# Feed-forward gate and linear part in three rounded passes instead of float32, in one phase of a four-layer model

## The chip, the cores and the metric

The kernel runs on one core of a Trainium2 chip. The metric is the device time of one execution in microseconds (us). A profiled execution also has a span, from its first recorded instruction to its last, and of this span the hardware profiler keeps every instruction of five engines: PE (TensorE, with PEld for its weight loads), DVE (VectorE), ACT (ScalarE), POOL (GpSimd) and SP (SyncE, which here issues transfers).

## The reference

Four layers run on 8 sequences of 512 tokens with 128 channels. The change is in the second half of the first layer, a small transformer of six layers, each an attention over windows of 32 tokens with 16 heads, followed by this feed-forward part (DIM 128, hidden width 341):

```python
def ffn_layer(x, g, bln, W1, b1, W2, b2):
    mu = x.mean(-1, keepdims=True)
    var = ((x - mu) ** 2).mean(-1, keepdims=True)
    xn = (x - mu) / jnp.sqrt(var + 1e-05) * g + bln
    hg = xn @ W1 + b1                       # 128 -> 682
    a, gate = jnp.split(hg, 2, -1)          # linear part, gate
    return a * jax.nn.gelu(gate, approximate=False) @ W2 + b2
```

All inputs and outputs are float32.

## The kernel before, in words

The phase concerned is `local_transformer_phase`. Six layers of 8 sequences of 4 tiles of 128 tokens give 192 tiles, and each engine runs one written-out loop `for k in range(-2, ALL + 8)`, whose order is the order of the program on that engine. Semaphores that are counted up per tile or per sequence tie the engines together; an engine waits in program order, so that all behind a wait stands still with it. In iteration k the kernel scores tile k, projects values for k+1 and queries and keys for k+2, and finishes k-1.

The feed-forward part of sequence n is spread over iterations: with t = k % 4, the sequence just ended is turned at t == 1 (`ffn_turn`), gets mean and deviation at t == 1 and 2 (`ffn_stats`, `ffn_shift`), and at t == 3 is turned back (`ffn_back`), scaled by ACT (`scale_norm`, which writes `xn`, 128 channels x 512 tokens) and multiplied with the gate half of W1 (`ffn_gate`). The linear half (`ffn_a`) follows at t == 0, the product with W2 at t == 1 and 2. Both halves have 341 columns in chunks of 128, 128 and 85 (`HCH`): the first chunk stands ahead of the second half of the attention-weighted values (`weigh_values(k, 1)`), the other two behind it.

At t == 3 the order is as follows, and the names are those used below. PE: scores, `ffn_back`, projections, `turn_out`, projection of keys, `turn_probs` (waits for ACT's exponentials), `turn_qk` (waits for `copy_out` of ACT), `weigh_values` first half, `project_out`, gate chunk 0, `weigh_values` second half, gate chunks 1 and 2, and then the scores of the next iteration. ACT: `scale_norm`, `square`, `exponentials`, `copy_out`, `square`, `copy_probs`, two `copy_qk`, `gelus`. DVE: `centre`, two `products`, `sum_squares`, `divide`, `sum_squares`, `add_output`, `divide`. POOL: `normalise` and then `rotate` for keys and queries, four additions of 128x512 that start when PE's `turn_qk` is through.

Float32 operands of a matmul count as one instruction in the program and leave two records in the trace. The projections of this phase already work in another way: `product` makes three matmuls of operands in the format float32r (`F32R`), of which one is a rounded value (hi) and the other its remainder (lo): hi x hi, hi x lo and lo x hi. ACT rounds (`nc.scalar.copy` to an F32R tile), and DVE or POOL subtracts to get the remainder.

W1 of a layer comes by one transfer in `load_ffn`, issued in the seventh iteration of a layer after the last sequence of the layer before is done, and `scale_norm` waits for it.

Of the kernel before, what the change touches and what calls it, by code (L numbers as in the profile page):

```python
# [8 lines left out]
F32 = mybir.dt.float32  # L9
# [7 lines left out]
P = 128  # L17
SEQS = 8
# [1126 lines left out]
def local_transformer_phase(nc, g, name, w):  # L1145
# [20 lines left out]
    def body(ph):  # L1166
# [4 lines left out]
        wo = sb("wo", [P, CH, P])  # L1171
        w1 = sb("w1", [P, 2 * HIDDEN])
        w2 = sb("w2", [P, 3, P])
# [32 lines left out]
        y_hat = sb("y_hat", [P, TOKENS])  # L1206
        xn = sb("xn", [P, TOKENS])
        gates = sb("gates", [P, 3, TOKENS])
        table_pick = sb("table_pick", [P, 3])
        bank = ph.ps("bank", [P, 8, TOKENS])  # L1210
# [6 lines left out]
        per_seq = {"ffn_turned": 1, "ffn_back": 1, "gate_done": 3, "a_done": 3, "w2_done": 2,  # L1217
                   "ys_hi_ready": 1, "y_tok_ready": 1, "xn_ready": 1, "gelu_done": 3,
                   "stats_ready": 1, "aggregated": 1, "var_ready": 1, "y_hat_ready": 1, "shift_ready": 1, "prod_ready": 3, "seq_done": 2,
# [3 lines left out]
        vals_loaded = [ph.sem(f"vals_loaded{i}") for i in range(2)]  # L1223
        split_hi, split_lo = ph.sem("split_hi"), ph.sem("split_lo")
        masks_ready, tables_ready, pads_ready = ph.sem("masks_ready"), ph.sem("tables_ready"), ph.sem("pads_ready")
        CONST_LOADS, FFN_LOADS = 16 * 4, 16 * 11
        PE_MADE = ("scores_done", "v_projected", "qk_projected", "probs_turned", "qk_turned", "out_turned", "pv_done", "wo_done",
                   "ffn_turned", "ffn_back", "gate_done", "a_done", "w2_done")
        ACT_MADE = ("exp_done", "v_copied", "squared", "probs_t_ready", "qkt_copied", "out_copied", "ys_hi_ready", "y_tok_ready", "y_hat_ready", "xn_ready", "gelu_done",
                    "logs_ready", "inv_norms_ready")  # L1230
        DVE_MADE = ("max_ready", "centred", "products_ready", "norms_ready", "sums_inverted", "att_ready", "y_added",
                    "stats_ready", "aggregated", "var_ready", "shift_ready", "prod_ready", "seq_done")
        POOL_MADE = ("rotated", "norms_guarded", "qk_normed", "ys_ready", "rstd_ready")
# [43 lines left out]
        with nc.Block() as block:  # L1277

            @block.sync
            def _(sp):  # L1280
# [13 lines left out]
                def load_ffn(layer):  # L1294
                    sp.wait_ge(q["seq_done"], seq("seq_done", layer * SEQS - 1))
                    sp.dma_start(w1[:], w["W1"][layer]).then_inc(ffn_loaded, 16)
                    sp.dma_start(w2[:, 0:2], w["W2"][layer, 0:2 * P].rearrange("(c p) d -> p c d", p=P)).then_inc(ffn_loaded, 16)
                    sp.dma_start(w2[0:HIDDEN - 2 * P, 2], w["W2"][layer, 2 * P:HIDDEN]).then_inc(ffn_loaded, 16)
                    for i, key in enumerate(("ln_g", "ln_b", "b2")):
                        sp.dma_start(ln[:, i:i + 1], w[key][layer].unsqueeze(1)).then_inc(ffn_loaded, 16)  # L1300
                    for side in range(2):
                        at = side * HIDDEN
                        sp.dma_start(b1[:, 3 * side:3 * side + 2], w["b1"][layer, at:at + 2 * P].rearrange("(c p) -> p c", p=P),
                                     allow_slow_non_contiguous=True).then_inc(ffn_loaded, 16)
                        sp.dma_start(b1[0:HIDDEN - 2 * P, 3 * side + 2:3 * side + 3], w["b1"][layer, at + 2 * P:at + HIDDEN].unsqueeze(1)).then_inc(ffn_loaded, 16)
                    sp.nop().then_inc(ffn_loaded, 16)
# [33 lines left out]
            def _(pe):  # L1340
# [145 lines left out]
                def ffn_back(n, k):  # L1486
# [4 lines left out]
                    last.then_inc(q["ffn_back"], 1)  # L1491

                def ffn_gate(n, k, chunks):
                    if 0 in chunks:
                        pe.wait_ge(q["xn_ready"], seq("xn_ready", n))
                        pe.wait_ge(ffn_loaded, FFN_LOADS * (n // SEQS + 1))
                        after_qk(k)
                    else:
                        pe.wait_ge(q["seq_done"], seq("seq_done", n - 1))
                    for i in chunks:  # L1500
                        h0, hn = HCH[i]
                        nc.tensor.matmul(bank[0:hn, FFN_HIDDEN[i], :], w1[:, HIDDEN + h0:HIDDEN + h0 + hn], xn[:], start=True, stop=True).then_inc(q["gate_done"], 1)

                def ffn_a(n, k, chunks):
                    if 0 in chunks:
                        after_qk(k)
                    for i in chunks:
                        h0, hn = HCH[i]
                        pe.wait_ge(q["gelu_done"], seq("gelu_done", n, i + 1))
                        nc.tensor.matmul(bank[0:hn, FFN_HIDDEN[i], :], w1[:, h0:h0 + hn], xn[:], start=True, stop=True).then_inc(q["a_done"], 1)  # L1510

# [49 lines left out]
            def _(act):  # L1561
# [62 lines left out]
                def copy_turned(n):  # L1624
                    act.wait_ge(q["ffn_turned"], seq("ffn_turned", n))
                    act.wait_ge(q["y_hat_ready"], seq("y_hat_ready", n - 1))
                    for odd in range(2):
                        last = nc.scalar.copy(y_tok[:].rearrange("p (t a d) -> p t a d", a=2, d=HD)[:, :, odd, :],
                                              bank[:, FFN_TURN[odd], 0:TILES * HD].rearrange("p (t d) -> p t d", d=HD))
                    last.then_inc(q["y_tok_ready"], 1)  # L1630
# [9 lines left out]
                def scale_norm(n):  # L1640
# [3 lines left out]
                    nc.scalar.activation(xn[:], bank[:, FFN_BACK, :], ACT.Identity, bias=ln[:, 1:2], scale=ln[:, 0:1]).then_inc(q["xn_ready"], 1)  # L1644

                def gelus(n):
                    nc.scalar.activation(table_pick[:, 1:2], table_pick[:, 0:1], ACT.Gelu)
                    act.wait_ge(q["w2_done"], seq("w2_done", n - 1))
                    for i, (h0, hn) in enumerate(HCH):
                        act.wait_ge(q["gate_done"], seq("gate_done", n, i + 1))  # L1650
                        nc.scalar.activation(gates[0:hn, i, :], bank[0:hn, FFN_HIDDEN[i], :], ACT.Gelu, bias=b1[0:hn, 3 + i:4 + i]).then_inc(q["gelu_done"], 1)
# [8 lines left out]
                for k in range(-2, ALL + 8):  # L1660
# [8 lines left out]
                    if is_tile(k):  # L1669
                        exponentials(k)  # L1670
                    if is_tile(k - 1):
                        copy_out(k - 1)
# [80 lines left out]
            def _(dve):  # L1753
# [65 lines left out]
                def ffn_stats(n):  # L1819
# [9 lines left out]
                    nc.vector.tensor_scalar(var_eps[:], mean_var[:, :, 1], LN_EPS, None, ALU.add).then_inc(q["var_ready"], 1)  # L1829

                def ffn_shift(n):
                    dve.wait_ge(q["rstd_ready"], seq("rstd_ready", n))
# [17 lines left out]
                for k in range(-2, ALL + 8):  # L1850
# [7 lines left out]
                    if t == 2 and is_seq(n - 1):  # L1858
                        ffn_shift(n - 1)
                    if is_tile(k):  # L1860
                        divide(k, 0)
# [599 lines left out]
```

## Time and profile before

| what | value |
|---|---|
| median of 3 runs | 4583.93 us (4583.06 to 4589.22) |
| the profiled execution, its own time | 4596.79 us |
| span of the profiled execution | 4595.0 us |
| PE busy over the span | 4112.4 us (89%) |
| DVE, ACT, POOL busy over the span | 3218.4, 2632.4 and 2429.1 us |

The phase with the change takes most of the span, roughly from 370 to 3560 us. A busy share is the time in which an engine works on something. For PE, records of matmuls overlap, since they are pipelined, so that the distance from one start to the next tells what a matmul costs, and not its recorded length. "Idle" is the time ahead of an instruction in which its engine had nothing to do, with what ended it. The columns of the rows are explained where they stand.

### The profile page before, as it was taken

Reading aid. Unit: us, or ns where it says so; the run is one execution under the profiler, and the core shown is the slowest. Engines: PE = TensorE matmul, PEld = TensorE weight load, DVE = VectorE, ACT = ScalarE, POOL = GpSimd, SP = SyncE. Lnnn points to the kernel's source line nnn. Section 1 sums busy time; section 2 is a strip of 40 time slices with the busy share of each in tenths; the row PEclk is TensorE's granted clock in tenths of the full one; section 3 lists DMA queues with packets and bytes.
Section 4 is the critical chain, followed back from the end, with each engine's and each line's share of the span. In section 5 each row is a group of like instructions: output and inputs, shape, how many; then the busy total and the mean of one; then the engine's idle time right before and its main releaser. Section 6 shows DMA issues by size and latency. Waiting matters only on the chain. (4 is left out here: it accounts for less than half of the span.)

```text
span 4595.0 us, 167423 instructions
## 1 busy us (share of the span) xinstructions
PE 4112.4 (89%) x70858; PEld 3335.7 (73%) x71050; DVE 3218.4 (70%) x5446; ACT 2632.4 (57%) x4318; POOL 2429.1 (53%) x1973
## 2 busy tenths in 40 slices
PE   6886999999999999999999999999998759668767
PEld 6885777777777777777777777777776449558457
DVE  4557777877778777877778777777775564564554
ACT  2324666666665666566666666666665437546445
POOL 3335665666566556656666566655663227517026
PEclk9997999999999999999999999999999869878878
DMA  1003222232222222232222222222221021221122
GB/s 27 0 0 92 68 68 69 58 90 69 69 66 78 69 68 67 61 85 71 67 70 77 71 67 68 70 62 70 68 66 44 10 64 49 72 63 44 28 67 77
DMA packets 214267, 281.83 MB, mean 61 GB/s; under 512 B 58926, under 2 KB 103764, under 8 KB 212788
## 3 DMA queue, kind: packets, MB, share of 16 engines
q1 hardware_dynamic: 199796, 249.82, 20.6%
q0 software_dynamic: 9536, 19.55, 1.6%
q8 instruction: 555, 9.09, 0.8%
q10 hardware_dynamic: 4224, 2.10, 0.2%
q14 instruction: 156, 1.28, 0.1%
HBM read 54.95 MB, written 18.28 MB: 16 GB/s over the span
## 5 line engine op out<-in xcount | busy, mean ns | idle before, releaser
L1717 POOL TENSOR_TENSOR local_normed<-local_rot,local_sines 128x512 f32<-128x512 f32 x768 | 954.8, 1279 | 837.4 <-PE local_bank L1429 832.9
L1727 POOL TENSOR_TENSOR local_normed<-local_normed,local_inv_norm 128x1024 f32<-128x1024 f32 x384 | 734.2, 1934 | 273.8 <-ACT local_inv_norm L1617 273.8
L1794 DVE TENSOR_TENSOR local_rot<-local_bank,local_table 128x1024 f32<-128x1024 f32 x384 | 470.2, 1224 | 399.9 <-ACT local_squares L1598 393.3
L1347 PE MATMUL local_bank<-local_wqkv_hi,local_ys_hi 128*128 128x512 f32 x1152 | 493.5, 428 | 33.9 <-issue 22.0
L1593 ACT COPY local_v_tile<-local_bank 128x1024 f32<-128x1024 f32 x192 | 195.1, 1016 | 545.0 <-PE local_bank L1349 545.0
L1794 DVE TENSOR_TENSOR local_sines<-local_bank,local_table 128x1024 f32<-128x1024 f32 x384 | 466.1, 1214 | 0.0
L1800 DVE TENSOR_REDUCE local_norm<-local_squares 128x16 f32<-128x1024 f32 x384 | 463.8, 1208 | 0.0
L1349 PE MATMUL local_bank<-local_wqkv_hi,local_ys_lo 128*128 128x512 f32 x1152 | 456.8, 397 | 0.0
L1348 PE MATMUL local_bank<-local_wqkv_lo,local_ys_hi 128*128 128x512 f32 x1152 | 454.7, 395 | 0.0
L1598 ACT ACTIVATE local_squares<-local_bank 128x1024 f32<-128x1024 f32 x384 | 397.0, 1034 | 76.9 <-PE local_bank L1349 76.9
L1781 DVE TENSOR_REDUCE local_top<-local_bank 128x16 f32<-128x1024 f32 x192 | 234.8, 1223 | 239.3 <-PE local_bank L1377 238.8
L1467 PE MATMUL local_bank<-local_att_t,local_wo 128*128 128x128 f32 x3072 | 391.6, 280 | 8.3 <-issue 2.9
L1467 PEld LDWEIGHTS local_bank<-local_att_t,local_wo 128*128 128x128 f32 x3072 | 359.2, 192 | 35.8 <-issue 18.1
L1429 PE MATMUL local_bank<-ident,local_normed 128*128 128x128 f32 x3072 | 374.1, 275 | 4.6 <-POOL local_normed L1727 4.1
L1455 PEld LDWEIGHTS local_bank<-local_vals,local_probs_t 64*32 64x32 f32 x24576 | 271.6, 105 | 138.9 <-issue 125.8
L1455 PE MATMUL local_bank<-local_vals,local_probs_t 64*32 64x65 f32 x24576 | 341.3, 225 | 18.9 <-issue 17.1
L1429 PEld LDWEIGHTS local_bank<-ident,local_normed 128*128 128x128 f32 x3072 | 334.0, 142 | 24.2 <-POOL local_normed L1727 5.2
L1377 PEld LDWEIGHTS local_bank<-local_k_t,local_q_t 64*32 64x32 f32 x24576 | 258.6, 105 | 115.0 <-issue 114.4
L1377 PE MATMUL local_bank<-local_k_t,local_q_t 64*32 64x64 f32 x24576 | 297.2, 226 | 25.6 <-issue 25.0
L1347 PEld LDWEIGHTS local_bank<-local_wqkv_hi,local_ys_hi 128*128 128x128 f32 x1152 | 219.2, 190 | 84.9 <-issue 36.0
L1810 DVE TENSOR_TENSOR local_att<-local_bank,local_inv_sum 128x512 f32<-128x512 f32 x384 | 265.4, 691 | 13.2
L1349 PEld LDWEIGHTS local_bank<-local_wqkv_hi,local_ys_lo 128*128 128x128 f32 x1152 | 219.0, 190 | 50.8
(406 smaller groups left out, 8821.5 us busy)
## 6 DMA issues: line engine op xcount, KB each, us to landing
local_vals<-local_v_tile SPq DMA_DIRECT2D x1152, 130.0 KB
local_vals<-local_v_tile SPq DMA_DIRECT2D x672, 65.0 KB
local_stage<-in_L_ffn_Wqkv SPq DMA_DIRECT2D x6, 1536.0 KB, 7.7
moe_w<-in_L_ffn_W SPq DMA_DIRECT2D x3, 2048.0 KB, 9.7
x_rows<-moe_rows SPq DMA_DIRECT2D x24, 256.0 KB, 4.6
moe_w<-y_rows SPq DMA_DIRECT2D x24, 256.0 KB, 5.3
local_wo<-in_L_ffn_Wo SPq DMA_DIRECT2D x6, 512.0 KB
moe_taken<-x_rows,moe_take POOLq DMA_INDIRECT x149, 2.6
```

What stands on the lines that cost most here:

```text
L1347: nc.tensor.matmul(out, hi, wqkv_hi[:, d0:d1], start=True, stop=False)
L1348: nc.tensor.matmul(out, hi, wqkv_lo[:, d0:d1], start=False, stop=False)
L1349: return nc.tensor.matmul(out, lo, wqkv_hi[:, d0:d1], start=False, stop=True)
L1377: last = nc.tensor.matmul(bank[b * BLOCK:(b + 1) * BLOCK, SCORES[odd], c * WIN:(c + 1) * WIN], q_t[rows, c, b * BLOCK:(b + 1) * BLOCK], k_ ...
L1429: last = nc.tensor.transpose(bank[:, QK_TURN[a][j // 4], j % 4 * P:(j % 4 + 1) * P], normed[:, (8 * a + j) * P:(8 * a + j + 1) * P], g.ide ...
L1455: last = nc.tensor.matmul(bank[b * BLOCK:(b + 1) * BLOCK, WEIGHED[i][odd], j * (HD + 1):(j + 1) * (HD + 1)], probs_t[rows, c, b * BLOCK:(b ...
L1467: last = nc.tensor.matmul(bank[:, WO_BANK, 0:P], wo[:, c, :], att_t[:, c, :], start=(c == 0), stop=(c == CH - 1))
L1598: nc.scalar.activation(squares[:, a * INNER:(a + 1) * INNER], two(QK[a]), ACT.Square).then_inc(q["squared"], 1)
L1717: last = nc.gpsimd.tensor_tensor(of_heads(normed, a)[:, :, to], of_heads(rot, a)[:, :, to], of_heads(sines, a)[:, :, of], ALU.add)
L1727: nc.gpsimd.tensor_tensor(of_heads(normed, a), of_heads(normed, a), inv_norm[:, a * HEADS:(a + 1) * HEADS].unsqueeze(2).to_broadcast([P, H ...
L1794: last = nc.vector.tensor_tensor(of_heads(out, a), src, table[:, m % TILES, row, :].unsqueeze(1).to_broadcast([P, HEADS, HD]), ALU.mult)
L1800: nc.vector.tensor_reduce(norm2[:, cols], of_heads(squares, a), AX, ALU.add).then_inc(q["norms_ready"], 1)
```

## The change

Gate and linear part are computed from split operands, as the projections are. Per sequence, ACT rounds `xn` into `xn_hi` and DVE writes the remainder `xn_lo` (`split_norm` on both); once in each of the six layers, at its first sequence, the same is done with W1 (`split_w1`). Each float32 matmul of `ffn_gate` and `ffn_a` becomes three (`in_three`). `xn` has no tile of its own any more and lies in `y_tok`; W1 is loaded into the tile of the gates. PE waits for the remainders ahead of gate chunk 0 (before: for `xn`).

```diff
-        w1 = sb("w1", [P, 2 * HIDDEN])
+        w1_hi, w1_lo = (sb(n, [P, 2 * HIDDEN], F32R) for n in ("w1_hi", "w1_lo"))
...
-        xn = sb("xn", [P, TOKENS])
+        xn = y_tok
+        xn_hi, xn_lo = (sb(n, [P, TOKENS], F32R) for n in ("xn_hi", "xn_lo"))
         gates = sb("gates", [P, 3, TOKENS])
+        w1 = gates[:].rearrange("p c t -> p (c t)")[:, 0:2 * HIDDEN]
...
+                def in_three(out, cols):
+
+                    nc.tensor.matmul(out, w1_hi[:, cols], xn_hi[:], start=True, stop=False)
+                    nc.tensor.matmul(out, w1_lo[:, cols], xn_hi[:], start=False, stop=False)
+                    return nc.tensor.matmul(out, w1_hi[:, cols], xn_lo[:], start=False, stop=True)
+
                 def ffn_gate(n, k, chunks):
                     if 0 in chunks:
-                        pe.wait_ge(q["xn_ready"], seq("xn_ready", n))
-                        pe.wait_ge(ffn_loaded, FFN_LOADS * (n // SEQS + 1))
+                        pe.wait_ge(q["xn_split"], seq("xn_split", n))
+                        pe.wait_ge(w1_split, n // SEQS + 1)
                         after_qk(k)
...
-                        nc.tensor.matmul(bank[0:hn, FFN_HIDDEN[i], :], w1[:, HIDDEN + h0:HIDDEN + h0 + hn], xn[:], start=True, stop=True).then_inc(q["gate_done"], 1)
+                        in_three(bank[0:hn, FFN_HIDDEN[i], :], slice(HIDDEN + h0, HIDDEN + h0 + hn)).then_inc(q["gate_done"], 1)
...
-                        nc.tensor.matmul(bank[0:hn, FFN_HIDDEN[i], :], w1[:, h0:h0 + hn], xn[:], start=True, stop=True).then_inc(q["a_done"], 1)
+                        in_three(bank[0:hn, FFN_HIDDEN[i], :], slice(h0, h0 + hn)).then_inc(q["a_done"], 1)
...
                 def copy_turned(n):
                     act.wait_ge(q["ffn_turned"], seq("ffn_turned", n))
                     act.wait_ge(q["y_hat_ready"], seq("y_hat_ready", n - 1))
+                    act.wait_ge(q["xn_split"], seq("xn_split", n - 1))
...
+                def split_norm(n):
+                    act.wait_ge(q["xn_ready"], seq("xn_ready", n))
+                    nc.scalar.copy(xn_hi[:], xn[:]).then_inc(q["xn_hi_ready"], 1)
+
+                def split_w1(layer):
+                    act.wait_ge(ffn_loaded, FFN_LOADS * (layer + 1))
+                    act.wait_ge(q["a_done"], seq("a_done", layer * SEQS - 1))
+                    nc.scalar.copy(w1_hi[:], w1).then_inc(w1_hi_ready, 1)
+
                 def gelus(n):
...
+                    if n % SEQS == 0:
+                        act.wait_ge(w1_split, n // SEQS + 1)
...
                     if is_tile(k):
                         exponentials(k)
+                    if t == 3 and is_seq(n - 1):
+                        split_norm(n - 1)
+                        if (n - 1) % SEQS == 0:
+                            split_w1((n - 1) // SEQS)
                     if is_tile(k - 1):
                         copy_out(k - 1)
...
+                def split_norm(n):
+                    dve.wait_ge(q["xn_hi_ready"], seq("xn_hi_ready", n))
+                    nc.vector.tensor_tensor(xn_lo[:], xn[:], xn_hi[:].bitcast(F32), ALU.subtract).then_inc(q["xn_split"], 1)
+
+                def split_w1(layer):
+                    dve.wait_ge(w1_hi_ready, layer + 1)
+                    nc.vector.tensor_tensor(w1_lo[:], w1, w1_hi[:].bitcast(F32), ALU.subtract).then_inc(w1_split, 1)
+
...
                     if t == 2 and is_seq(n - 1):
                         ffn_shift(n - 1)
+                    if t == 3 and is_seq(n - 1):
+                        split_norm(n - 1)
+                        if (n - 1) % SEQS == 0:
+                            split_w1((n - 1) // SEQS)
                     if is_tile(k):
                         divide(k, 0)
```

On ACT, at t == 3 of the first sequence of a layer, before the change (`local_xn` is the scaled row, `local_att_t` is what `copy_out` writes):

```order
L1644 ACTIVATE local_xn<-local_bank,local_ln 128x512
L1598 ACTIVATE local_squares<-local_bank 128x1024
L1586 ACTIVATE local_scores<-local_scores 128x1024
L1622 COPY local_att_t<-local_bank 128x1024
L1598 ACTIVATE local_squares<-local_bank 128x1024
```

and with the change, where the scaled row goes to `local_y_tok`:

```order
L1654 ACTIVATE local_y_tok<-local_bank,local_ln 128x512
L1607 ACTIVATE local_squares<-local_bank 128x1024
L1595 ACTIVATE local_scores<-local_scores 128x1024
L1658 CAST local_xn_hi<-local_y_tok 128x512
L1663 CAST local_w1_hi<-local_gates 128x682
L1631 COPY local_att_t<-local_bank 128x1024
L1607 ACTIVATE local_squares<-local_bank 128x1024
```

The rounding of the row stands between the exponentials and `copy_out`; in the other seven sequences of a layer the cast of 682 columns is not there. On DVE at the same place, with the change (before, the first and the fourth of these rows stand next to each other):

```order
L1825 TENSOR_REDUCE local_norm2<-local_squares 128x16
L1858 TENSOR_TENSOR local_xn_lo<-local_y_tok,local_xn_hi 128x512
L1862 TENSOR_TENSOR local_w1_lo<-local_gates,local_w1_hi 128x682
L1831 RECIPROCAL local_inv_sum<-local_bank 128x8
L1835 TENSOR_TENSOR local_att<-local_bank,local_inv_sum 128x2x4x64
```

The remainders follow the first `sum_squares`, which itself follows both `products`. On PE the gate before:

```order
L1467 MATMUL local_bank<-local_att_t,local_wo 128x128 x8
L1502 MATMUL local_bank<-local_xn,local_w1 128x512
L1455 MATMUL local_bank<-local_vals,local_probs_t 32x65 x32
L1502 MATMUL local_bank<-local_xn,local_w1 128x512
L1502 MATMUL local_bank<-local_xn,local_w1 85x512
L1370 MATMUL local_bank<-local_band8,local_ident16 128x512 x2
```

and with the change:

```order
L1470 MATMUL local_bank<-local_att_t,local_wo 128x128 x8
L1498 MATMUL local_bank<-local_xn_hi,local_w1_hi 128x512
L1499 MATMUL local_bank<-local_xn_hi,local_w1_lo 128x512
L1500 MATMUL local_bank<-local_xn_lo,local_w1_hi 128x512
L1458 MATMUL local_bank<-local_vals,local_probs_t 32x65 x32
L1498 MATMUL local_bank<-local_xn_hi,local_w1_hi 128x512
L1499 MATMUL local_bank<-local_xn_hi,local_w1_lo 128x512
L1500 MATMUL local_bank<-local_xn_lo,local_w1_hi 128x512
L1498 MATMUL local_bank<-local_xn_hi,local_w1_hi 85x512
L1499 MATMUL local_bank<-local_xn_hi,local_w1_lo 85x512
L1500 MATMUL local_bank<-local_xn_lo,local_w1_hi 85x512
```

Nothing has changed its place on PE; three instructions stand for one, and what the first of them waits for is another event.

## Rows read from the trace of the kernel before

**Rows 1.** Stretch, length; PE, PEld, DVE, ACT, POOL busy; granted clock, DMA share, GB/s.

```profile
500.00:3500.00 3000.00, 2913.09 (x60776) 2309.31 (x60960) 2331.92 (x3106) 1880.58 (x2530) 1815.38 (x1418) 1.00 0.27 70
```

**Rows 2.** Timeline of PE: start, length, line, out<-in, count, idle before.

```profile
1032.15 0.47 PE L1347 MATMUL local_bank<-local_wqkv_hi,local_ys_hi 128*128 128x512 f32 x1
1032.46 0.39 PE L1348 MATMUL local_bank<-local_wqkv_lo,local_ys_hi 128*128 128x512 f32 x1
1032.69 0.40 PE L1349 MATMUL local_bank<-local_wqkv_hi,local_ys_lo 128*128 128x512 f32 x1
...
1034.77 1.94 PE L1429 MATMUL local_bank<-ident,local_normed 128*128 128x128 f32 x16
...
1037.52 2.02 PE L1467 MATMUL local_bank<-local_att_t,local_wo 128*128 128x128 f32 x16
1039.38 1.02 PE L1502 MATMUL local_bank<-local_xn,local_w 128*128 128x512 f32 x2
1040.33 0.86 PE L1455 MATMUL local_bank<-local_vals,local_probs_t 64*32 64x65 f32 x64
1041.12 1.98 PE L1502 MATMUL local_bank<-local_xn,local_w 128*128 128x512 f32 x4
1042.09 0.59 PE L1502 MATMUL local_bank<-local_xn,local_w 128*85 128x512 f32 x1
1042.52 0.59 PE L1502 MATMUL local_bank<-local_xn,local_w 128*85 128x512 f32 x1
1043.16 0.38 PE L1370 MATMUL local_bank<-local_band,local_ident 128*128 128x512 bf16 x1
...
1057.30 1.98 PE L1510 MATMUL local_bank<-local_xn,local_w 128*128 128x512 f32 x4
1059.33 0.38 PE L1370 MATMUL local_bank<-local_band,local_ident 128*128 128x512 bf16 x1
```

**Rows 3.** Timeline of ACT in the same iteration.

```profile
1032.66 1.07 ACT L1586 ACTIVATE local_scores<-local_scores 128x1024 f32<-128x1024 f32 x1
1033.61 1.02 ACT L1622 COPY local_att_t<-local_bank 128x1024 f32<-128x1024 f32 x1
1034.50 1.06 ACT L1598 ACTIVATE local_squares<-local_bank 128x1024 f32<-128x1024 f32 x1
```

**Rows 4.** Two lines of the expert phases: count, shortest/median/longest ns, first and last start.

```profile
L285 ACT CAST moe_wt_hi<-moe_w x149: 617/619/657, 3784.9 to 4564.6; 128x512 fp32r x149
...
L569 DVE TENSOR_TENSOR moe_wt_lo<-moe_w,moe_wt_hi x149: 691/692/766, 3787.1 to 4565.3; 128x512 fp32r<-128x512 f32 x149
```

**Rows 5.** Timeline of DVE in the iteration of rows 2.

```profile
1037.86 1.21 DVE L1800 TENSOR_REDUCE local_norm<-local_squares 128x16 f32<-128x1024 f32 x1
1038.98 0.20 DVE L1806 RECIPROCAL local_inv_sum<-local_bank 128x8 f32<-128x8 f32 x1
```

**Rows 6.** The line of `ffn_shift` on DVE, columns as in rows 4.

```profile
L1833 DVE SCALAR_TENSOR_TENSOR local_shift<-local_mean_var,local_rstd x48: 161/760/949, 498.5 to 3545.9; 128x4 f32<-128x4 f32 x48
```

**Rows 7.** Timeline of DVE and POOL, at t == 2 and t == 3.

```profile
1024.38 0.77 DVE L1833 SCALAR_TENSOR_TENSOR local_shift<-local_mean_var,local_rstd 128x4 f32<-128x4 f32 x1
...
1021.39 4.97 POOL L1717 TENSOR_TENSOR local_normed<-local_rot,local_sines 128x512 f32<-128x512 f32 x4 [2.10 <-PE local_bank L1429]
...
1035.98 4.98 POOL L1717 TENSOR_TENSOR local_normed<-local_rot,local_sines 128x512 f32<-128x512 f32 x4 [4.04 <-PE local_bank L1429]
```

**Rows 8.** Timeline of DVE and POOL where the projection weights are split.

```profile
371.16 3.49 DVE L1775 TENSOR_TENSOR local_wqkv_lo<-local_stage,local_wqkv_hi 128x1024 fp32r<-128x1024 f32 x3
...
1401.77 5.76 DVE L1775 TENSOR_TENSOR local_wqkv_lo<-local_stage,local_wqkv_hi 128x1024 fp32r<-128x1024 f32 x2
...
1401.58 4.87 POOL L1727 TENSOR_TENSOR local_normed<-local_normed,local_inv_norm 128x1024 f32<-128x1024 f32 x2
```

**Rows 9.** An idle time of PE, and the stretch behind it, columns as in rows 1.

```profile
1553.29 0.68 PE L1377 MATMUL local_bank<-local_k_t,local_q_t 64*32 64x64 f32 x44 [2.10 <-issue]
...
1555.00:1558.00 3.00, 3.00 (x8) 2.32 (x7) 1.45 (x2) 0.98 (x2) 0.00 (x0) 0.50 0.00 0
```

More of the change, by code:

```diff
@@ L1217, in body @@
         per_seq = {"ffn_turned": 1, "ffn_back": 1, "gate_done": 3, "a_done": 3, "w2_done": 2,
-                   "ys_hi_ready": 1, "y_tok_ready": 1, "xn_ready": 1, "gelu_done": 3,
+                   "ys_hi_ready": 1, "y_tok_ready": 1, "xn_ready": 1, "xn_hi_ready": 1, "xn_split": 1, "gelu_done": 3,
                    "stats_ready": 1, "aggregated": 1, "var_ready": 1, "y_hat_ready": 1, "shift_ready": 1, "prod_ready": 3, "seq_done": 2,
@@ L1224, in body @@
         split_hi, split_lo = ph.sem("split_hi"), ph.sem("split_lo")
+        w1_hi_ready, w1_split = ph.sem("w1_hi_ready"), ph.sem("w1_split")
         masks_ready, tables_ready, pads_ready = ph.sem("masks_ready"), ph.sem("tables_ready"), ph.sem("pads_ready")
@@ L1228, in body @@
                    "ffn_turned", "ffn_back", "gate_done", "a_done", "w2_done")
-        ACT_MADE = ("exp_done", "v_copied", "squared", "probs_t_ready", "qkt_copied", "out_copied", "ys_hi_ready", "y_tok_ready", "y_hat_ready", "xn_ready", "gelu_done",
+        ACT_MADE = ("exp_done", "v_copied", "squared", "probs_t_ready", "qkt_copied", "out_copied", "ys_hi_ready", "y_tok_ready", "y_hat_ready", "xn_ready", "xn_hi_ready", "gelu_done",
                     "logs_ready", "inv_norms_ready")
         DVE_MADE = ("max_ready", "centred", "products_ready", "norms_ready", "sums_inverted", "att_ready", "y_added",
-                    "stats_ready", "aggregated", "var_ready", "shift_ready", "prod_ready", "seq_done")
+                    "xn_split", "stats_ready", "aggregated", "var_ready", "shift_ready", "prod_ready", "seq_done")
         POOL_MADE = ("rotated", "norms_guarded", "qk_normed", "ys_ready", "rstd_ready")
@@ L1295, in load_ffn @@
                     sp.wait_ge(q["seq_done"], seq("seq_done", layer * SEQS - 1))
-                    sp.dma_start(w1[:], w["W1"][layer]).then_inc(ffn_loaded, 16)
+                    sp.dma_start(w1, w["W1"][layer]).then_inc(ffn_loaded, 16)
                     sp.dma_start(w2[:, 0:2], w["W2"][layer, 0:2 * P].rearrange("(c p) d -> p c d", p=P)).then_inc(ffn_loaded, 16)
```

## The prediction

> **What bounds the kernel now.** I read the busy times by stretch first. In the phase with the change PE works 2913 of 3000 us at the full granted clock (1.00, that is 2.4 GHz), and DVE, the next, 2332 [rows 1]. So here nearly every microsecond that PE gains or stands still is one of the kernel, unless another engine is late right behind it. Next I read the timelines of one iteration with t == 3, which I take for all 48. The reader is to see how close ACT is to PE there: `copy_out` (L1622) ends at 1033.61 + 1.02 = 1034.63, and PE's `turn_qk` (L1429) starts at 1034.77 [rows 2, 3]. It is released by that copy, with 0.14 us from the end of the one to the start of the other. Ahead of the gate there is little room on DVE too: the first `sum_squares` gives way to the next instruction at 1038.98, and PE starts the gate at 1039.38 [rows 2, 5].
>
> **What the matmuls save.** In each half (gate, linear part) the two PE stretches take 1040.33 - 1039.38 = 0.95 us for one matmul (two records) and 1043.16 - 1041.12 = 2.04 us for two; in the linear part the latter is 1059.33 - 1057.30 = 2.03 [rows 2]. Together 2.99 us, of which six records at a spacing of 0.43 (1042.09 to 1042.52) are 2.58 and 0.41 are changeovers: 0.09 behind the first stretch, 0.11 at the head of the second, 0.21 behind it.
>
> The projections show three-pass matmuls of the same 128x512 shape: 0.31 us from the first start to the next, then 0.23 [rows 2]. With three and six passes that is 0.31 + 2 x 0.23 = 0.77 and 0.31 + 5 x 0.23 = 1.46, together 2.23 if no other changeover is left. If 0.09 and 0.21 behind them stay (they belong to what follows: small weight tiles, then bf16), and the second head costs 0.03 more, it is 2.56. So a half gains 0.43 to 0.76 us, a sequence 0.87 to 1.5, and 48 sequences 42 to 73 us. I take 0.88 a sequence: the gaps are in the trace at just these two places, and nothing shows them to go. That the last chunk is 85 wide changes nothing, as its records are as far apart as the others'.
>
> **The rounding on ACT.** 48 casts of 128x512, each between the exponentials and `copy_out`. The same cast in the expert phases takes 617 ns [rows 4], and an ACT instruction starts about 0.1 us before the end of the one ahead (1034.50 against 1034.63) [rows 3], so 0.52 us of ACT's time; the bounds are 0.5 and 0.64. Queued behind it are `copy_out`, the second `square`, `copy_probs` and both `copy_qk`. PE waits for the first of these already, so `turn_qk` and all behind it start 0.52 us later: PE reaches the gate at 1039.90. DVE's second `products` wait for the second `square`, so `sum_squares` shifts by 0.52 as well, and POOL's `rotate`, released by `turn_qk`, too.
>
> **The remainder on DVE.** The subtraction may start at 1038.98 + 0.52 = 1039.50 and takes 0.69 us where POOL leaves it alone [rows 4]. Here POOL is in `rotate`. Where DVE reads two SBUF operands against POOL, the trace shows what happens: `ffn_shift`, four elements wide, has a median of 760 ns and a minimum of 161 [rows 6]. It starts 2.99 us into `rotate` and ends at 1025.15 [rows 7], that is 3.76 in, or 3.60 before its own 0.16: it had to wait until the third of POOL's four additions was over. The split of the projection weights says the same: three subtractions of 128x1024 take 3.49 us without POOL, and two take 5.76 beside two operations of POOL, the first of which began 0.19 us ahead of them [rows 8]. Our subtraction starts 1039.50 - (1035.98 + 0.52) = 3.00 us into `rotate`, at the very place of `ffn_shift` one iteration earlier. It gets its turn 3.60 us in, at 1040.10, ends at 1040.79, and PE, 0.14 later, starts the gate at 1040.93 instead of 1039.90: a wait of 1.03 us. The bounds of this wait: 0.43 with no contention (0.69 in place of 1.29), and 1.7 if DVE has to stand by for one whole addition of 1.25 us.
>
> The Trainium skill says on "SBUF — State Buffer", section "SBUF: two separate sides", that the port pair of DVE and GpSimd is "an exclusive lock, not a bandwidth split": who starts first keeps it for the whole instruction. The trace agrees: 4 elements cost 0.6 us more, which a shared bandwidth would not do. Were the ports shared in proportion, the subtraction would take half of the weights' 2.9 us and the wait would be 1.2 us, which adds 7 us to the sum below.
>
> Behind the gate DVE still has `divide`, `sum_squares`, `add_output` and `divide`, some 3.2 us, before the next scores, for which PE needs 0.86 + 0.79 + 1.69 = 3.3 us from the gate; the half of `divide` that the scores wait for comes first. I count nothing there, nor for the shared tiles: `y_tok` is read by DVE long before `xn` overwrites it, W1 arrives under the same wait and as early as before, and the new waits of `copy_turned` and `gelus` are met before ACT comes to them: the one a whole iteration earlier, the other by the gate that `gelus` waits for in any case.
>
> **A usual sequence.** 0.52 + 1.03 - 0.88 = +0.67 us; 42 of them +28 us.
>
> **The first sequence of a layer (6 of them).** ACT also casts 682 columns of W1: 0.65 us more (between 0.52 for 512 and some 0.95 for 1024), so `turn_qk` is 1.17 late and PE is at the gate at 1040.55. DVE ends the row's remainder at 1040.79 + 0.65 = 1041.44. POOL's fourth addition (1.25 us) has been waiting and takes its turn; then W1 needs 0.87 (682 columns, between 0.69 and 1.16), to about 1043.5, and PE starts at 1043.65: a wait of 3.1 us (1.3 without contention). PE after such a stop: behind an idle time of 2.10 us the granted clock lies at 0.50 (1.2 GHz) over a whole 3 us [rows 9], which costs half of some 3.4 us, 1.7 us. Sum 1.17 + 3.1 + 1.7 - 0.88 = 5.1, six times +31 us.
>
> **Sum.** +28 + 31 = +59 us, less about 5 where PE comes to the gate late anyway by an idle time of its instruction supply, as in rows 9. The profiled 4596.79 us would become 4651; the median of the runs lies 12.9 below that execution, so I predict 4583.93 + 54 = 4638 us.
>
> **Rivals.**
> - The forecast, 0.62: PE waits twice in each iteration with t == 3; 4615 to 4665.
> - Both waits as forecast, but the changeovers vanish (1.5 a sequence) and the clock holds. Against it: the gaps and the clock seen. 42 x 0.05 + 6 x 2.8 = +19, so 4603. 0.15.
> - DVE takes its operands at once. For it: the subtraction is short. Against it: the wait of four elements [rows 6, 7]. 42 x (0.52 + 0.43 - 0.88) + 6 x (1.17 + 1.3 - 0.88) = +3 + 10, so 4597, or 4567 with the larger gain of the matmuls. 0.09.
> - Faster: both stops are made good behind the gate, because PE would have stood still there anyway (for its instructions, or for DVE at the next scores), and the gain of the matmuls alone is left: 4511 to 4542. It decides if PE has 1.5 us of idle time per sequence to give. For it: PE is idle for 87 of 3000 us [rows 1], some 1.9 in each 65. Against it: in the iteration shown the start of each group follows the one ahead without a gap from 1037.52 to 1043.16 [rows 2]. 0.08.
> - Much slower: the clock falls in each sequence, as two stops of 0.5 and 1.0 us lie close together. Against it: it is the full clock over the stretch in spite of many idle times near 1 us. 42 x 1.7 = +71 more, 4709. 0.06.
>
> **How the numbers follow.** 4638 is the likeliest case. The range for 8 in 10 runs from 4594, just below the case without contention, to 4668, which is the upper bound of DVE's wait (42 x 0.67 = 28 more). A measurement of this kernel can tell 0.2%, 9 us, from no change. Faster by more: 0.09 (the fourth rival and a corner of the third). Within it: 0.09 (most of the third, and a part of the second). Slower: 0.82.
>
> **What would show it.** In the profile of the changed kernel, at t == 3: nine matmul records per half, 0.23 us apart; PE's `turn_qk` released by ACT's `copy_out`, whose start lies 1.47 us behind that of the exponentials (now 0.95); the subtraction of 128x512 on DVE near 1.3 us long and not 0.69; an idle time of PE of about 1 us ahead of the first gate matmul, released by DVE, 48 times, and near 3 us in six of them, with a lower clock behind; PE's total idle time in the phase up by some 75 us and its busy time down by 40. I am wrong if the subtraction takes 0.7 us, if PE does not wait at the gate, or if the linear part, too, gets a wait.

## The result, and the profile after

The changed kernel takes 4645.35 us (median of 4 runs, 4639.33 to 4651.82), the kernel before beside it 4583.58 us (4583.06 to 4589.22). The ratio is 1.0121 with a 95% interval of 1.0104 to 1.0138: slower by 62 us, and 7 us above the forecast time of 4638. The profiled execution of the changed kernel took 4649.19 us, with a span of 4647.4 us.

The three-pass products sit at L1498, L1499 and L1500, for the gate as for the linear part. The rounding of `local_xn` on ACT is L1658 and that of W1 L1663; the remainders on DVE are L1858 and L1862. Other lines have moved: `turn_qk` is L1432 (was L1429), `copy_out` L1631 (L1622), the scores begin at L1373 (L1370).

The first view is that of busy times from 500 to 3500 us, with the columns of [rows 1].

```profile
500.00:3500.00 3000.00, 2841.33 (x59808) 2313.95 (x59971) 2345.38 (x3102) 1871.62 (x2533) 1802.72 (x1391) 0.99 0.28 68
```

In the same 3000 us PE is busy for 72 us less than in [rows 1], so it stands still for 72 us more. DVE gains 13 us and is still far from full: nothing is short of capacity, PE only stands still more often. The waits say where. They follow for PE from 500 to 3620 us: what waited, for what, us in total, times, longest.

```profile
PE local_bank L1498 <- DVE local_xn_lo L1858: 32.2, 39, 2.3
PE local_bank L1432 <- ACT local_att_t L1631: 23.4, 47, 1.1
PE local_bank L1498 <- issue: 16.1, 6, 2.7
```

Together they make 71.7 us, and none of the three stood among the waits before. `turn_qk` waits for `copy_out` in 47 sequences, and the gate for DVE's remainder. The third row is the first sequence of each of six layers; the wait there is for DVE as well (below), although the view puts it down to PE's own issue.

A usual sequence on PE follows, with start, duration, engine, line, operation and operands; the bracket is the idle time ahead and what ended it.

```profile
1115.56 1.09 PE L1419 MATMUL local_bank<-ident,local_scores 128*128 128x128 f32 x8
1117.07 1.94 PE L1432 MATMUL local_bank<-ident,local_normed 128*128 128x128 f32 x16 [0.42 <-ACT local_att_t L1631]
1118.94 0.86 PE L1458 MATMUL local_bank<-local_vals,local_probs_t 64*32 64x65 f32 x64
1119.81 2.02 PE L1470 MATMUL local_bank<-local_att_t,local_wo 128*128 128x128 f32 x16
1122.63 0.50 PE L1498 MATMUL local_bank<-local_xn_hi,local_w_hi 128*128 128x512 f32 x1 [0.80 <-DVE local_xn_lo L1858]
1122.97 0.39 PE L1499 MATMUL local_bank<-local_xn_hi,local_w_lo 128*128 128x512 f32 x1
1123.20 0.40 PE L1500 MATMUL local_bank<-local_xn_lo,local_w_hi 128*128 128x512 f32 x1
1123.53 0.86 PE L1458 MATMUL local_bank<-local_vals,local_probs_t 64*32 64x65 f32 x64
1124.32 0.50 PE L1498 MATMUL local_bank<-local_xn_hi,local_w_hi 128*128 128x512 f32 x1
```

The row of L1432 answers to `turn_qk` in [rows 2], which had no idle time ahead that the view shows, and that of the first L1498 to the first L1502. From `project_out` (L1470) to the gate it was 1.86 us; it is 2.82 here. In the linear part of the same sequence nothing waits, and the same distance is shorter than before, 1.78 us:

```profile
1136.57 2.02 PE L1470 MATMUL local_bank<-local_att_t,local_wo 128*128 128x128 f32 x16
1138.35 0.48 PE L1498 MATMUL local_bank<-local_xn_hi,local_w_hi 128*128 128x512 f32 x1
...
1141.28 0.40 PE L1500 MATMUL local_bank<-local_xn_lo,local_w_hi 128*85 128x512 f32 x1
1141.75 0.38 PE L1373 MATMUL local_bank<-local_band,local_ident 128*128 128x512 bf16 x1
```

So the wait at the gate is 2.82 - 1.78 = 1.04 us; against the gate's place in the kernel before it is 2.82 - 1.86 = 0.96. Next ACT, DVE and POOL in the same iteration, which answer to [rows 3], [rows 5] and [rows 7].

```profile
1114.44 1.06 ACT L1595 ACTIVATE local_scores<-local_scores 128x1024 f32<-128x1024 f32 x1
1115.39 0.63 ACT L1658 CAST local_xn_hi<-local_y_tok 128x512 fp32r<-128x512 f32 x1
1115.90 1.03 ACT L1631 COPY local_att_t<-local_bank 128x1024 f32<-128x1024 f32 x1
```

```profile
1120.16 1.21 DVE L1825 TENSOR_REDUCE local_norm<-local_squares 128x16 f32<-128x1024 f32 x1
1121.28 1.29 DVE L1858 TENSOR_TENSOR local_xn_lo<-local_y_tok,local_xn_hi 128x512 fp32r<-128x512 f32 x1
1122.50 0.20 DVE L1831 RECIPROCAL local_inv_sum<-local_bank 128x8 f32<-128x8 f32 x1
```

```profile
1118.29 5.43 POOL L1742 TENSOR_TENSOR local_normed<-local_rot,local_sines 128x512 f32<-128x512 f32 x4 [5.48 <-PE local_bank L1432]
```

The rounding moves `copy_out` from 0.95 to 1.46 us behind the exponentials. The subtraction starts 2.99 us into POOL's four additions, is 1.29 us long and ends 4.28 us in; the additions themselves go from 4.98 to 5.43 us.

In the first sequence of a layer DVE has the remainder of W1 behind that of the row, and PE starts the gate at its end:

```profile
1052.30 1.29 DVE L1858 TENSOR_TENSOR local_xn_lo<-local_y_tok,local_xn_hi 128x512 fp32r<-128x512 f32 x1
1053.52 1.92 DVE L1862 TENSOR_TENSOR local_w_lo<-local_gates,local_w_hi 128x682 fp32r<-128x682 f32 x1
```

```profile
1050.83 2.02 PE L1470 MATMUL local_bank<-local_att_t,local_wo 128*128 128x128 f32 x16
1055.53 0.77 PE L1498 MATMUL local_bank<-local_xn_hi,local_w_hi 128*128 128x512 f32 x1 [2.68 <-issue]
1056.10 0.63 PE L1499 MATMUL local_bank<-local_xn_hi,local_w_lo 128*128 128x512 f32 x1
1056.52 0.63 PE L1500 MATMUL local_bank<-local_xn_lo,local_w_hi 128*128 128x512 f32 x1
```

The subtraction of W1 ends at 1055.44 and the gate begins at 1055.53, 4.70 us behind `project_out`. Its passes lie 0.42 apart and not 0.23: the clock is at its lower level (0.50, that is 1.2 GHz), as the windows (length, PE busy, granted clock, DMA share, GB/s) show.

```profile
1054.00:1056.00 2.00, 0.47 (x1) 0.75 0.00 0
1056.00:1058.00 2.00, 2.00 (x67) 0.50 0.00 0
1058.00:1060.00 2.00, 2.00 (x24) 0.50 0.14 33
1060.00:1062.00 2.00, 1.75 (x12) 0.54 0.19 42
```

### The profile page after: what moved, and what is told of

It is laid out like the page before. It is cut to its first block and busy times, and to the rows that moved or that the text cites. A ratio compares the mean times of both kernels' runs of the same rounds, so it can differ in the third digit from the quotient of the medians.

```text
span 4647.4 us, 168115 instructions
## 1 busy us (share of the span) xinstructions
PE 4094.8 (88%) x71146; PEld 3391.0 (73%) x71338; DVE 3279.4 (71%) x5500; ACT 2660.0 (57%) x4372; POOL 2448.6 (53%) x1973
## 3 DMA queue, kind: packets, MB, share of 16 engines
q1 hardware_dynamic: 199796, 249.82, 21.3%
q14 instruction: 157, 1.29, 0.1%
## 5 line engine op out<-in xcount | busy, mean ns | idle before, releaser
L1742 POOL TENSOR_TENSOR local_normed<-local_rot,local_sines 128x512 f32<-128x512 f32 x768 | 976.3, 1305 | 849.7 <-PE local_bank L1432 845.2
L1470 PE MATMUL local_bank<-local_att_t,local_wo 128*128 128x128 f32 x3072 | 394.7, 282 | 10.8 <-DMA local_wo<-in_L_ffn_Wo 4.5
L1432 PE MATMUL local_bank<-ident,local_normed 128*128 128x128 f32 x3072 | 375.0, 275 | 27.8 <-ACT local_att_t L1631 23.4
L1470 PEld LDWEIGHTS local_bank<-local_att_t,local_wo 128*128 128x128 f32 x3072 | 362.3, 193 | 37.3 <-issue 10.1
L1432 PEld LDWEIGHTS local_bank<-ident,local_normed 128*128 128x128 f32 x3072 | 335.0, 142 | 52.3 <-issue 33.1
```

The costliest lines, as they stand in the source:

```text
L1432: last = nc.tensor.transpose(bank[:, QK_TURN[a][j // 4], j % 4 * P:(j % 4 + 1) * P], normed[:, (8 * a + j) * P:(8 * a + j + 1) * P], g.ide ...
L1470: last = nc.tensor.matmul(bank[:, WO_BANK, 0:P], wo[:, c, :], att_t[:, c, :], start=(c == 0), stop=(c == CH - 1))
L1742: last = nc.gpsimd.tensor_tensor(of_heads(normed, a)[:, :, to], of_heads(rot, a)[:, :, to], of_heads(sines, a)[:, :, of], ALU.add)
```

## The experiments

For each kernel the table has the distances between the starts of the scores (the first bf16 mask matmul that the trace records) of one tile and of the next, read from PE's timeline of the profiled execution, and summed: 47 tiles with the gate, 47 with the linear part (the first of each lies ahead of the first gate), and 96 others. It keeps apart where time goes, which a median of whole runs can't. The others differ by up to 11 us from before, with both signs, so single digits there mean little. A profiled execution can also lie up to 13 us from the median of its kernel (before: 4596.79 against 4583.93; remainder early: 4569.69 against 4582.48), so the sums and the ratios need not agree to 10 us.

| kernel | with gate | with linear part | others | sum | ratio to before (95%) |
|---|---|---|---|---|---|
| before | 825.4 | 761.6 | 1516.9 | 3103.9 | |
| changed | 897.9 | 740.3 | 1523.4 | 3161.6 | 1.0121 (1.0104 to 1.0138) |
| passes alone | 809.0 | 741.7 | 1517.7 | 3068.4 | 0.9932 (0.9919 to 0.9945) |
| cast alone | 851.7 | 760.9 | 1509.2 | 3121.8 | 1.0055 (1.0042 to 1.0067) |
| remainder early | 829.1 | 741.7 | 1516.6 | 3087.4 | 0.9998 (0.9989 to 1.0007) |
| W1 once | 877.3 | 741.6 | 1518.3 | 3137.2 | 1.0091 (1.0078 to 1.0104) |
| cast early | 867.3 | 741.8 | 1527.1 | 3136.2 | 1.0068 (1.0052 to 1.0083) |
| both early | 798.0 | 745.5 | 1528.2 | 3071.7 | 0.9924 (0.9910 to 0.9938) |
| norm early, old passes | 818.9 | 761.8 | 1513.1 | 3093.8 | 0.9979 (0.9970 to 0.9989) |

The median of the kernel before was 4584.29 us beside the first four experiments (17 runs) and 4592.1 beside the last three (17 runs), so ratios are the better comparison across the two.

The theory under test is that of the prediction: cheaper products (about -40 us), against two separate waits, one behind the rounding on ACT and one for the remainder on DVE, the latter long because POOL works beside it. The rivals are that the products gain nothing here, that one wait covers the other, or that the slower first sequences are what counts.

**Passes alone.** The three passes stay, what feeds them goes: ACT scales the row straight into `xn_hi`, no remainder of it is made, the third pass takes `xn_hi` again, and PE waits for the scaled row as it did before. So the output is not the full one.

```
-    return nc.tensor.matmul(out, w1_hi[:, cols], xn_lo[:], ...)
+    return nc.tensor.matmul(out, w1_hi[:, cols], xn_hi[:], ...)
...
-    nc.scalar.activation(xn[:], bank[:, FFN_BACK, :], ...)
+    nc.scalar.activation(xn_hi[:], bank[:, FFN_BACK, :], ...)
...
-    split_norm(n - 1)              # ACT and DVE
-    if (n - 1) % SEQS == 0:
+    if n - 1 == 0:
         split_w1(...)
```

> The three passes alone: ACT scales the row straight into the rounded tile, no remainder of the row is made (the third pass multiplies the rounded row again), and W1 is split in the first layer only and then kept; so remainders and the later layers' W1 are left out. My theory: PE gains 0.37 us in the gate and 0.46 in the linear part of each sequence and nothing stands against it, 48 x 0.83 = 40 us below the kernel before, 4544 us; no idle time of PE ahead of the gate, turn_qk as before at 0.14 us behind copy_out. Rival one (changeovers vanish without the waits): 73 us below, 4511. Rival two (the gain is swallowed by another wait behind the gate or by the supply of instructions): 4580 or more.

Measured: 4555.84 us, 28 us below before by the medians and 31 by the ratio (interval 25 to 37), so less than expected. In the trace the sum of the tiles falls by 35.5: 16.4 with the gate, 19.9 with the linear part, nothing in the others. Once, in layer 0, the split of W1 is still in it. That the products are faster on the chip is shown; the expected 40 us lie just above the interval.

**Cast alone.** The kernel before, and ACT writes a rounded `local_xn` that nobody reads.

```
...
+    def split_norm(n):
+        act.wait_ge(q["xn_ready"], seq("xn_ready", n))
+        nc.scalar.copy(xn_hi[:], xn[:])
...
+    if t == 3 and is_seq(n - 1):
+        split_norm(n - 1)          # between exponentials and copy_out
```

> The kernel before with nothing but a cast of the row on ACT, 128x512, between the exponentials and copy_out, into a tile that nobody reads. My theory: PE's turn_qk is released by copy_out and starts 0.52 us later in each of 48 sequences, which nothing behind gives back: 25 us above the kernel before, 4609 us. Rival (the stop is made good at a later wait): 4584 us, with idle times of PE that shrink behind turn_qk.

Measured: 4610.65 us, +26. The added row among PE's waits, in which `turn_qk` is L1430 and `copy_out` L1623:

```profile
PE local_bank L1430 <- ACT local_att_t L1623: 19.2, 47, 0.4
```

A rounding of 0.62 us on an engine that is busy for 57% of the span costs PE 26.3 us in the tiles with the gate, 0.57 for each of 46 gates among them. One bare instruction does it, with no remainder and no new semaphore on PE.

**Remainder early.** All of the change, but DVE takes both remainders between the two pairs of rotate products, where POOL is idle.

```
...
     products(k + 2, 0)
+    if t == 3 and is_seq(n - 1):
+        split_norm(n - 1)
+        if (n - 1) % SEQS == 0:
+            split_w1((n - 1) // SEQS)
...
     products(k + 2, 1)
     sum_squares(k + 2, 0)
...
-    (the same four lines)
```

> The changed kernel with DVE's remainders (row, and W1 in the first sequence of a layer) moved from behind sum_squares to between the two products, where POOL's rotate has not begun; ACT's casts stay. Theory of the lock: the subtraction of 128x512 takes 0.69 us instead of 1.29, lies in a time in which DVE waits for ACT's square, PE no longer waits at the gate (0.79 us of idle time 42 times and 2.68 six times go, and with the latter the half clock): 42 x 0.98 + 6 x 4.5 = 68 us below the changed kernel, 4577 us. Rival one (the subtraction is long by itself, whatever POOL does): 1.29 us here too, second products 0.3 us late, about the same time. Rival two (PE waits for something else at the gate as well): 4610 us or more.

Measured: 4582.48 us (4569.69 to 4594.67, 12 runs), no change from before. The two subtractions by themselves (count, shortest/median/longest in ns), first as the change has them:

```profile
L1858 DVE TENSOR_TENSOR local_xn_lo<-local_y_tok,local_xn_hi x48: 692/1290/1300, 514.8 to 3607.3; 128x512 fp32r<-128x512 f32 x48
L1862 DVE TENSOR_TENSOR local_w_lo<-local_gates,local_w_hi x6: 1914/1916/1917, 516.0 to 3192.8; 128x682 fp32r<-128x682 f32 x6
```

and in the kernel with them early:

```profile
L1858 DVE TENSOR_TENSOR local_xn_lo<-local_y_tok,local_xn_hi x48: 679/681/694, 509.4 to 3530.2; 128x512 fp32r<-128x512 f32 x48
L1862 DVE TENSOR_TENSOR local_w_lo<-local_gates,local_w_hi x6: 860/861/861, 510.0 to 3121.9; 128x682 fp32r<-128x682 f32 x6
```

The same instructions on the same data take 0.68 instead of 1.29 us and 0.86 instead of 1.92. The changed kernel says the same by itself: its shortest, 0.69 us, are those of the last two sequences, whose subtraction stands at its usual place in the program, but with no addition of POOL beside it, since no keys and queries are left to rotate. The first of the two:

```profile
3577.60 0.69 DVE L1858 TENSOR_TENSOR local_xn_lo<-local_y_tok,local_xn_hi 128x512 fp32r<-128x512 f32 x1 [1.63 <-ACT local_xn_hi L1658]
```

In the kernel with the remainders early the wait at the gate is gone from every sequence but one, and the other one is left untouched:

```profile
PE local_bank L1432 <- ACT local_att_t L1631: 23.4, 47, 1.1
...
PE local_bank L1498 <- DVE local_xn_lo L1858: 2.3, 1, 2.3
```

By the medians 63 us of the changed kernel's time are gone, and the tiles with the gate give back 68.8 us in the profiled execution, which is this kernel's shortest. So the two waits are separate.

**W1 once.** The change with W1 rounded and its remainder taken in layer 0 alone, so that later layers use stale parts of W1 and the output is not the full one; the waits for the split of W1 ask for the first split alone.

```
...
-    if (n - 1) % SEQS == 0:        # ACT and DVE
+    if n - 1 == 0:
         split_w1((n - 1) // SEQS)
```

> The changed kernel with W1 split in the first layer only (the later layers reuse that split, so their W1 is left out); the row is split in every sequence. My theory: five of the six long stops go. Each costs 0.66 us at turn_qk, 1.9 at the gate and 1.1 to 2.3 by the half clock behind it, 4.3 on average: 22 us below the changed kernel, 4623 us. Rival (the clock would have fallen anyway or costs nothing): 5 x 2.6 = 13 us below, 4632.

Measured: 4626.48 us, 19 below the changed kernel by the medians. The tiles with the gate are 20.6 us shorter, and the five of them that begin a later layer 23.0, 4.6 each. The first sequences are a third of the loss and not all of it: 42 us over before remain.

**Cast early.** All of the change, with ACT's part of it ahead of `copy_v`, where ACT stands idle for about 2 us; DVE's remainders where the change put them.

```
+    if t == 3 and is_seq(n - 1):
+        scale_norm(n - 1)
+        split_norm(n - 1)
+        if (n - 1) % SEQS == 0:
+            split_w1((n - 1) // SEQS)
     if is_tile(k + 1):
         copy_v(k + 1)
...
-    (the same lines behind, and split ahead of copy_out)
```

> The changed kernel with ScalarE's move alone: rounding of local_xn and W1 ahead of copy_v, VectorE's remainders left where the change put them (behind the second square sums, beside GpSimd's rotate additions). The whole output is computed. Theory (two separate stops that add up): the stop at turn_qk (23.4 us) goes, the one of the gate on the remainder (72 us of idle in all, 48 times about 1.0 to 1.5 more than before) stays: 4645 - 24 = about 4621 us. Rival (one stop covers the other): with turn_qk earlier, VectorE's queue is no earlier, the gate waits that much longer, and the time stays within 8 us of 4645.

Measured: 4627.49 us, a ratio of 1.0068 where the change had 1.0121, so 24 us less by the ratios (18 by the medians, whose kernel before was 8 us slower here), as the first theory has it; the wait of `turn_qk` is gone, and the gate's is as it was:

```profile
PE local_bank L1498 <- DVE local_xn_lo L1858: 31.8, 40, 2.3
...
PE local_bank L1498 <- issue: 15.9, 6, 2.7
```

In five of the six first sequences the subtraction starts earlier against POOL's additions here, 2.64 us in instead of 3.00. It is 1.65 us long instead of 1.29 and ends where it did, 4.29 in:

```profile
1041.63 5.39 POOL L1742 TENSOR_TENSOR local_normed<-local_rot,local_sines 128x512 f32<-128x512 f32 x4 [6.81 <-PE local_bank L1432]
...
1044.27 1.65 DVE L1858 TENSOR_TENSOR local_xn_lo<-local_y_tok,local_xn_hi 128x512 fp32r<-128x512 f32 x1
```

So its end goes by the place in POOL's row and not by its own start.

**Both early.** Both moves together.

> The changed kernel with both moves: ScalarE writes local_xn, its rounding and (in the first sequence of a layer) W1's rounding ahead of copy_v, where ScalarE sits idle about 2 us, so that nothing stands between the exponentials and copy_out; VectorE takes both remainders between the two pairs of rotate products of an earlier place, where GpSimd's additions are not running. The whole output is computed. Theory (the two stops are all that the change costs): the stop at turn_qk goes too, 23.4 us in the remainder-early kernel, and of its 4582.5 us 23 leave: 4559 us; by its profiled run, which was its shortest (4569.7), 4546; so 4546 to 4562, faster than the kernel before. Rival (ScalarE is full, the cast only moves its delay to copy_v and the squares): copy_v and what follows come 0.5 to 1.5 us later, PE waits there as long as it did at turn_qk, and the time stays at 4575 to 4590.

Measured: 4557.1 us (4550.98 to 4563.07), ratio 0.9924. It is the faster version with the whole output. Neither wait is left; for the remainder PE waits once:

```profile
PE local_bank L1498 <- DVE local_xn_lo L1858: 2.3, 1, 2.3
```

**Norm early, old passes.** The kernel before, with `scale_norm` alone ahead of `copy_v`.

```
+    if t == 3 and is_seq(n - 1):
+        scale_norm(n - 1)
     if is_tile(k + 1):
         copy_v(k + 1)
```

> The kernel before (four-pass float32 products, no split) with one move alone: ScalarE writes local_xn ahead of copy_v instead of just ahead of the square and the exponentials. It prices the move itself. Theory: copy_out is met 0 to 0.2 us earlier in 48 sequences, so 4574 to 4584 us, and most of what the both-early kernel gains is then the passes' own. Rival: if the move alone gave 25 us or more (4560 or less), the gain of the both-early kernel would be an order's and not the change's.

Measured: 4581.24 us, ratio 0.9979. So the order alone is worth 0.2%, and of the 0.76% of the kernel with both moves 0.9924 / 0.9979 = 0.9945, some 25 us, belong to the three passes. By the table they return 20.9 us with the gate and 16.3 with the linear part, and the other tiles take 15.1 back. Both kernels with the early rounding have the highest sums there (1527 and 1528). PE waits 4.4 us for `copy_v`'s tile where the old passes have 2.0, which is only a part of it:

```profile
PE local_bank L1443 <- ACT local_v_tile L1602: 4.4, 6, 1.2
```

Whether the later `copy_v` costs the rest was not tried and stays open.

## Why the prediction was right

**What bounds the kernel.** PE's time was the kernel's, and ACT was right behind it at `turn_qk`. Both held: the cast alone cost its full 0.52 us, 48 times (25 us forecast, 26 measured), and none of it was made good further on.

**The matmuls.** Forecast: 0.88 us a sequence. In the timelines a gate half takes 0.90 us for one product and 1.72 for two, 2.62 in place of 2.99, a gain of 0.37; the linear half gains as much and 0.08 ahead of it. That is 0.83, at the low end of 0.87 to 1.5 and just under it. The 0.09 behind the first product did not vanish, it is 0.10 now. The 0.21 behind the second was misread: it is no changeover. Each tile has two mask matmuls, and the traces of the kernels before and changed have the record of one alone (192 records, but 384 of their weight loads). So the 0.47 us from the last pass to the mask matmul (1141.28 to 1141.75) hold a matmul that is not recorded. The trace of the kernel with the remainder early has both, and the first of them follows at the distance of one pass, 0.23:

```profile
1168.54 0.39 PE L1500 MATMUL local_bank<-local_xn_lo,local_w_hi 128*85 128x512 f32 x1
1168.77 0.61 PE L1373 MATMUL local_bank<-local_band,local_ident 128*128 128x512 bf16 x2
```

Those 0.21 us could not go, so the forecast's upper bound of 1.5 us a sequence was 0.4 too high. The term itself was sized right, because its low end kept every gap that the trace showed, this one for a reason that was not quite the true one. In the whole stage it is 36 rather than 40 (28 by the medians).

**The rounding on ACT.** Forecast: +0.52 us, copy 1.47 us behind the exponentials. Seen: 1.46, and +26 us by itself.

**The remainder on DVE.** Forecast: start 3.00 us into POOL's additions, end 4.29 in, wait 1.03. Seen: 2.99, 4.28 and, counted as the forecast does from the gate's place before, 0.96. The rival without contention (4597) fell with the 1.29 us of the row of L1858, and the run with the remainder early shows that the length is POOL's doing and not the instruction's. The rule named in the prediction, that the port goes to one engine for a whole instruction ("SBUF — State Buffer", "SBUF: two separate sides", of the Trainium skill), agrees with this pair: 0.61 us are added to a subtraction of 0.68, and 1.06 to one of 0.86, which is no fixed ratio. The cast-early kernel bears it out too: a subtraction that starts 0.36 us earlier in POOL's row ends no earlier.

**The sum of a usual sequence.** Forecast: +0.67. In the trace the 40 tiles of usual gates are 39.9 us longer than before, +1.00 each, and tiles with the linear part 0.47 shorter: +0.53. The median gate tile is +1.09, which gives +0.62, near the forecast. The mean is lower because PE of the kernel before sometimes stood still for its own issue where that of the changed one did not: the three gate tiles that came out 0.9 to 1.3 us shorter had 1.62 to 1.77 us of such idle time before and 0 to 0.71 after.

**The first sequence of a layer.** Forecast: a stop of 3.1, half a clock for 1.7, in all +5.1. Seen: the six tiles with the gate take 143.7 us in place of 110.6, +5.5 each, less 0.47, so +5.0. `turn_qk` is 1.17 us late, as forecast (`copy_out` starts 2.12 us behind the exponentials, 0.95 before). The other pieces differ and make up for each other, so that the good sum is partly luck. The stop is 4.70 - 1.86 = 2.84 us (2.68 by the view), not 3.1, since W1's remainder takes 1.92 and not the 2.1 from 1.25 of POOL and 0.87 of its own. The clock stays low for longer in two of the six, some 6.8 us in the windows above, so that it costs 2.3 us on average and not 1.7.

**The rest.** Added over the tiles, the gates make +72.5, the linear parts -21.3 and the others +6.5, 57.7 in all, where the sum ahead of the last step was +59 and the forecast +54. The 5 us taken off for sequences in which PE is late anyway are about what the mean of the usual ones lies below its forecast, 42 x 0.14 = 6. The other tiles' +6.5 stand in no term of the forecast and are within what such sums differ by from kernel to kernel. 4638 was 7 below the median. The upper end of the range, 4668, is 4666 by its own sum; nothing hangs on it.

**The rivals.** That the stops are made good behind the gate fell: no stop came back. That the changeovers vanish and the clock holds fell by the 0.10 us above and by the lower clock behind all six long stops. That the clock falls in every sequence fell too: with both waits in them, the usual sequences are +1.00 us at the gate, with no room for another 1.7, and no stretch at the lower clock lies in one of the 40 usual gate tiles.

## What to carry to other kernels

Splitting operands makes the matmul cheaper and gives the elementwise engines two new instructions per operand; ask of each what is queued behind it, since here 0.6 us a sequence on an engine that is busy for 57% of the span cost 26 us, where the matmuls gave some 28 to 36. Before putting a VectorE instruction with two SBUF operands on the path, look what GpSimd does in those very microseconds: the same subtraction took 0.68 or 1.29 us. The repair is the order and not the arithmetic: with the rounding and the remainder moved into idle time ahead, the same arithmetic made the kernel 0.8% faster (0.2% of it the order's own) instead of 1.2% slower.

## What the runs showed of the hardware beside this

The stretches at the lower clock came in two sizes. From 500 to 3500 us, in windows of 2 us, (1 - clock) x 2 us adds up to 25.6 us in the changed kernel and 13.7 in the one before. Each stretch makes about 1.7 us of it (3.4 us at half clock) or twice that: 11 and 2 of them after, 4 and 2 before. The windows below are one of the short kind, in the first layer, those at 1054 us above are one of the long (6.8 us). Why a stop of 2.7 us is followed by the one or the other was not settled.

```profile
518.00:520.00 2.00, 1.97 (x68) 0.78 0.00 0
520.00:522.00 2.00, 2.00 (x5) 0.50 0.26 61
522.00:524.00 2.00, 1.93 (x93) 0.87 0.06 14
```

A stop on DVE's work was not always put down to DVE: all six waits for W1's remainder stand under PE's issue (16.1 us, 6 times), and only the end of L1862, 0.09 us ahead of the gate, tells what they were.
